# An eight-stage GNN, expert, LSTM and attention kernel: attention weights chosen by address, softmax sums by a ones column, query tiles outside; four more LSTM matmuls per cell issued ahead

## The reference

```
logits = sel_in @ W_sel.T + b_sel
onehot = one_hot(argmax(logits), 4)
g = einsum('bsg,bs->bg', g_all, onehot)
h2, c2 = _lstm_activate(g, c)
```

```
logits = relu(x.mean(axis=1) @ r_w1 + r_b1) @ r_w2 + r_b2
sel = argmax(softmax(logits))
scores = einsum('bhqd,bhkd->bhqk', q, k) / sqrt(64)
out = einsum('bhqk,bhkd->bhqd', softmax(scores), v) ... @ wo
```

## Time and profile before

| | |
|---|---|
| runs, median (lowest to highest) | 5700.91 us (5697.95 to 5701.5) |
| the profiled execution's own time | 5706.91 us |
| its span | 5705.1 us |
| PE busy | 5027.5 us, 88% |
| DVE busy | 2837.5 us, 50% |
| ACT busy | 1437.0 us, 25% |
| LSTM steps | from about 2110 to 4963 us |
| attention and store | 5384 to 5705 us |

### The profile page before, as it was taken

One profiled execution on the slowest core, in us unless ns is written; L12 is line 12 of the kernel. 1 busy time (PEld: TensorE's weight loads), 2 busy tenths in 40 slices (PEclk: granted clock), 3 DMA queues, 4 the chain that ended last, 5 costly groups with the idle time before them and its releaser, 6 DMA issues. The chain is left out here.

```text
span 5705.1 us, 267215 instructions
## 1 busy us (share of the span) xinstructions
PE 5027.5 (88%) x109528; PEld 3080.5 (54%) x109528; DVE 2837.5 (50%) x11506; ACT 1437.0 (25%) x4745; POOL 633.6 (11%) x1073
## 2 busy tenths in 40 slices
PE   8899686899998989999999999999999999777688
PEld 6644343444565446666666666666666666554444
DVE  4501344232554755555555555555555555574533
ACT  0000000012332343333333333333333333242222
POOL 0000382000662110000000000000000000021000
PEclk9899897999999989999999999999999999898877
DMA  0000111166444740000000000000000000000200
GB/s 11 15 30 15 30 42 31 56 240 240 125 120 144 258 129 12 10 10 12 10 10 10 12 10 10 12 11 10 10 12 10 10 12 10 19 15 36 74 12 9
DMA packets 157671, 265.00 MB, mean 46 GB/s; under 512 B 48686, under 2 KB 83636, under 8 KB 153241
## 3 DMA queue, kind: packets, MB, share of 16 engines
q1 hardware_dynamic: 102548, 181.63, 9.6%
q0 software_dynamic: 55040, 82.30, 5.1%
HBM read 178.38 MB, written 85.14 MB: 46 GB/s over the span
## 5 line engine op out<-in xcount | busy, mean ns | idle before, releaser
L1558 PE MATMUL bank<-lstm_w,step_h_parts 128*32 128x128 f16 x87360 | 1453.8, 220 | 241.8 <-issue 241.8
L1558 PEld LDWEIGHTS bank<-lstm_w,step_h_parts 128*32 128x32 f16 x87360 | 1238.4, 97 | 613.3 <-issue 349.3
L1629 DVE TRANSPOSE_TENSOR_REDUCE step_summed<-bank 128x4 f32 (+1 forms) x2500 | 792.4, 317 | 1085.2 <-PE bank L1558 914.5
L1553 PE MATMUL bank<-step_xg,step_rows 128*128 (+1 forms) x2500 | 757.7, 385 | 45.1 <-DMA step_xg<-lstm_xg 18.8
L1526 ACT ACTIVATE step_act_out<-step_summed,lstm_inv_scale 128x4 f32<-128x4 f32 x625 | 185.8, 297 | 1724.1 <-DVE step_summed L1629 1724.1
L1514 POOL COPY xnT<-step_state 128x4 f32 (+1 forms) x625 | 116.7, 187 | 2759.9 <-DVE step_state L1654 2759.9
L1179 PE MATMUL bank<-sum_parts,sum_hot 125*125 125x512 f16 x1600 | 346.9, 380 | 6.7 <-DVE sum_parts L1138 6.7
L1179 PEld LDWEIGHTS bank<-sum_parts,sum_hot 125*125 125x125 f16 x1600 | 219.0, 137 | 135.0 <-DVE sum_parts L1138 7.5
L1429 PE MATMUL bank<-xg_w,xnT 128*125 128x512 f32 x640 | 276.6, 595 | 6.7 <-DMA xg_w<-in_c_w_ih 6.7
L538 POOL DMA_INDIRECT gcn_rows<-gcn_h_rows,gcn_idx x160 | 202.5, 1265 | 703.3 <-issue 703.3
L1553 PEld LDWEIGHTS bank<-step_xg,step_rows 128*128 128x128 bf16 x2500 | 142.5, 97 | 167.7 <-issue 129.8
(11 more groups left out here) (370 smaller groups left out, 6369.6 us busy)
## 6 DMA issues: line engine op xcount, KB each, us to landing
rel_h<-rel_h_sb SPq DMA_DIRECT2D x39, 1024.0 KB, 6.4
lstm_xg<-cnt POOLq DMA_DIRECT2D x80, 375.0 KB, 3.7
step_xg<-lstm_xg SPq DMA_DIRECT2D x375, 80.0 KB
xg_w<-in_c_w_ih SPq DMA_DIRECT2D x16, 1024.0 KB
lstm_w<-in_c_w_hh SPq DMA_DIRECT2D x16, 1024.0 KB, 11.6
cheb_w<-in_L_gnn_weight SPq DMA_DIRECT2D x8, 1024.0 KB
choose_we<-in_L_ffn_experts SPq DMA_DIRECT2D x8, 1024.0 KB
rel_bases<-in_L_gnn_bases SPq DMA_DIRECT2D x8, 1024.0 KB, 11.4
```

What stands on the lines that cost most here:

```text
L1553: return nc.tensor.matmul(bank[:], rows[:, p, :], xg[:, at, :], start=True, stop=stop)
L1558: last = nc.tensor.matmul(bank[32 * q:32 * q + 32, 128 * s:128 * s + 128], h_parts[:, c, :], w[:, s, c, q, a, 128 * p:128 * p + 128], star ...
L1629: nc.vector.tensor_reduce(summed[:, 4 * p:4 * p + 4], bank[:, bass.ds(s * 128, 128)].rearrange("p (b r) -> p b r", r=32), X_AXIS, ALU.add, ...
```

## The change

**LSTM.** 32 matmuls instead of 16 are issued before the choice: both halves of the first h piece, for each cell. The chosen cell then has 120 left instead of 124. `inject_i_o` moves behind them.

**Attention.** The three candidates of each weight are laid out on the host as one array, widened to 8 heads (`c_wq`, `c_wk`, `c_wv`, `c_wo`). SP waits for the index, loads it into a register and fetches only the chosen matrices, k first. One-hot, mixing and ring are gone. `v` gets a 65th column of ones for each head, so that `sum_values(i)` (ten passes with 65 columns for each tile) gives the row's sum beside its values. `expo` no longer sums, `normalize` is gone, and `keep_sums` divides 64 columns by the sum behind the matmul. Query tiles are the outer loop, heads the inner one. Each query tile is turned, projected, added and stored while the next runs; `store` as a stage is gone.

```diff
 def cell(s):
     for part in parts:
-        for c, a in halves[1 if part is part_f else 0:]:
+        for c, a in halves[2 if part is part_f else 0:]:
...
 last.then_inc(score_done, 1)
-inject_i_o(t)
 pe.wait_ge(h_lo_ready, t)
 for s in range(CELLS):
-    add_half(part_f, s, 0, 0, stop=False)
+    for a in range(2):
+        add_half(part_f, s, 0, a, stop=False)
+inject_i_o(t)
 pe.wait_ge(picked, 1)
```

```diff
-TILES = [(hd, m) for hd in range(AH) for m in range(NT)]
+TILES = [(hd, m) for m in range(NT) for hd in range(AH)]
+P_SLOTS = 3
...
 # sync
-for n, (w, i) in enumerate(PAIRS):
...
+sp.wait_ge(picked, 1)
+e = sp.value_load(pick[0:1, 0:1], min_val=0, max_val=NK - 1)
+def load(name, dst, loaded):
+    sp.dma_start(dst[:], I[name].rearrange("e (c p) n -> p (e c) n", p=128)[:, bass.ds(e * KC, KC), :]
+                 ).then_inc(loaded, 16)
+load("c_wk", wk, wk_loaded)
+load("c_wq", wq, wq_loaded)
+load("c_wv", wv, wv_loaded)
+load("c_wo", wo, wo_loaded)
+for m in range(NT):
+    sp.wait_ge(added, m + 1)
+    sp.dma_start(B.out_rows[:, m, :], B.x[:, m, :]).then_inc(out_stored, 16)
+sp.wait_ge(out_stored, 16 * NT)
...
 # vector
-def normalize(i):
...
+def keep_sums(i):
+    hd, m = TILES[i]
+    s = slice(i % 4, i % 4 + 1)
+    dve.wait_ge(o_done, i + 1)
+    nc.vector.reciprocal(inv[:, s], sums[:, DK:DK + 1]).then_inc(inv_ready, 1)
...
+    nc.vector.tensor_scalar(o[:, m % 2, hd * DK:(hd + 1) * DK], sums[:, 0:DK], inv[:, s], None, ALU.mult
+                            ).then_inc(o_kept, 1)
+for i in range(M + 1):
+    if i < M:
+        keep_turned(i)
+    if i + 2 < M:
+        row_max(i + 2)
+    if i >= 1:
+        keep_sums(i - 1)
+    if i >= AH and i % AH == 6:
+        add_out(i // AH - 1)
...
 # tensor
-def sum_head(hd):
...
+def sum_values(i):
+    hd, m = TILES[i]
+    pe.wait_ge(pT_kept_a, i + 1)
+    pe.wait_ge(pT_kept_v, i + 1)
+    if i >= 1:
+        pe.wait_ge(o_kept, i)
+    for t in range(NT):
+        last = nc.tensor.matmul(sums, pT[:, i % 2, t, :], v[:, t, hd, :], start=(t == 0),
+                                stop=(t == NT - 1))
+    last.then_inc(o_done, 1)
+def turn_out(m):      # four transposes of o into bank 7
...
+def project(m):
+    pe.wait_ge(oT_kept, m + 1)
+    for c in range(KC):
+        last = nc.tensor.matmul(B.bank[7][0:R, :], oT[:, m % 2, c, :], wo[:, c, :], start=(c == 0),
+                                stop=(c == KC - 1))
+    last.then_inc(out_done, 1)
+for i in range(M + 1):
+    if i < M:
+        turn(i)
+    if i + 2 < M:
+        scores(i + 2)
+    if i >= 1:
+        sum_values(i - 1)
+    if i >= AH and i % AH == 2:
+        turn_out(i // AH - 1)
+    if i >= AH and i % AH == 4:
+        project(i // AH - 1)
```

More of the change, by code:

```diff
@@ L2188, in _ @@
[L2188 to L2205, removed]
+            nc.vector.max_index(pick[:], best[:], score[:]).then_inc(picked, 1)
@@ L2246, in _ @@
-            for i in range(M + 2):
-                if i >= 2:
-                    keep_turned(i - 2)
-                    if (i - 2) % NT == 1 and i - 2 > NT:
-                        keep_out((i - 2) // NT - 1)
-                if 1 <= i <= M:
-                    normalize(i - 1)
-                if i < M:
-                    row_max(i)
-            keep_out(AH - 1)
-            for m in range(NT):
-                dve.wait_ge(out_done, m + 1)
-                nc.vector.tensor_tensor(B.x[:, m, :], B.x[:, m, :], B.bank[m % 4][0:R, :], ALU.add
-                                        ).then_inc(added, 1)
+            def keep_turned(i):
+                dve.wait_ge(p_turned, i + 1)
+                if i >= 2:
+                    dve.wait_ge(o_done, i - 1)
+                nc.vector.tensor_copy(pT[:, i % 2, 4, :], turn_tail).then_inc(pT_kept_v, 1)
@@ L2278, in expo @@
[L2278 to L2281 removed]
+                if i >= P_SLOTS:
+                    act.wait_ge(p_turned, i - P_SLOTS + 1)
@@ L2306, in _ @@
+            expo(1)
+            for i in range(M):
+                keep_turned(i)
+                if i + 2 < M:
+                    expo(i + 2)
+                if i >= AH and i % AH == 2:
+                    keep_oT(i // AH - 1)
+            keep_oT(NT - 1)
         @block.tensor
@@ L2378, in _ @@
+            def project(m):
+                pe.wait_ge(oT_kept, m + 1)
+                for c in range(KC):
+                    last = nc.tensor.matmul(B.bank[7][0:R, :], oT[:, m % 2, c, :], wo[:, c, :], start=(c == 0),
+                                            stop=(c == KC - 1))
+                last.then_inc(out_done, 1)
             scores(0)
             scores(1)
-            for i in range(M):
-                turn(i)
+            pe.wait_ge(v_kept, NT + 1)
+            pe.wait_ge(wo_loaded, 16)
@@ L2382, in _ @@
+            for i in range(M + 1):
+                if i < M:
+                    turn(i)
                 if i + 2 < M:
                     scores(i + 2)
-                if i % NT == 0 and i > 0:
-                    sum_head(i // NT - 1)
-            sum_head(AH - 1)
-            pe.wait_ge(o_kept, 2 * AH)
-            pe.wait_ge(w_mixed, 4 * NK)
-            for m in range(NT):
-                if m >= 4:
-                    pe.wait_ge(added, m - 3)
-                for c in range(KC):
-                    last = nc.tensor.matmul(B.bank[m % 4][0:R, :], oT[:, c, m * R:(m + 1) * R], wmix[:, 3, c, :],
-                                            start=(c == 0), stop=(c == KC - 1))
-                last.then_inc(out_done, 1)
@@ L2398, in store @@
-def store(nc, ctx, B, out):
-    stored = nc.alloc_semaphore("out_stored")
-    with nc.Block() as block:
-        @block.sync
-        def _(sp):
-            sp.dma_start(out.rearrange("(j p) d -> p j d", p=R), B.x[:]).then_inc(stored, 16)
-            sp.wait_ge(stored, 16)
+                if i >= 1:
+                    sum_values(i - 1)
+                if i >= AH and i % AH == 2:
+                    turn_out(i // AH - 1)
+                if i >= AH and i % AH == 4:
+                    project(i // AH - 1)
@@ L2407, in program @@
+            turn_out(NT - 1)
+            project(NT - 1)
 def program(nc, I, out):
@@ L2417, in program @@
                 stage(nc, ctx, B)
-        store(nc, ctx, B, out)
 def lay_out(inputs):
@@ L2443, in lay_out @@
     out["c_xg_rows"] = rows
+    for name in "qkvo":
+        ws = [out.pop(f"L3_ffn_w{name}{i}") for i in range(3)]
+        out["c_w" + name] = np.stack([np.repeat(w.reshape(512, -1, 64), 512 // w.shape[1], 1).reshape(512, 512) for w in ws])
     w = out.pop("L2_ffn_W_sel")
```

188 lines of the change are left out of this document (78 added, 110 removed).

## The result

The changed kernel takes 5623.2 us (median of four runs, 5618.8 to 5623.8), against 5701.2 in the same session (5698.0 to 5705.0): a ratio of 0.986 with a 95% interval of 0.9845 to 0.9876, 78 us less. The forecast was 5644, with a range of 5600 to 5690. The profiled execution is the fastest of the four: 5618.8, span 5617.0, 88.1 less than the span before.

| part | before | after | difference | forecast |
|---|---|---|---|---|
| stages ahead of the LSTM | 1788.8 | 1782.7 | -6.1 | 0 |
| LSTM with its preparation | 3180.5 | 3164.5 | -16.0 | -5 |
| graph attention | 404.0 | 400.8 | -3.2 | 0 |
| attention, up to the first scores | 105.1 | 78.8 | -26.3 | -27 |
| loop and projection | 213.2 | 184.7 | -28.5 | -17 |

What follows compares the result with a forecast made beforehand. LSTM steps wait for the choice, and TensorE bounds the attention loop at a mean clock of 0.70. Terms -27 - 17 - 8 - 5 = -57 take the profiled 5706.9 to 5650, median 5644 us, range 5600 to 5690.

Steps and rivals of the forecast that it cites:

- Weights by address, -27: Attention before the loop: fetching only the chosen weights starts scores at 5451.5 instead of 5478.4, -27 us (-21 to -28).
- The bound on the other side: Attention weight fetch: k could take the store's 11.3 us if sharing queues with the other three; 5.3 was kept.
- The loop, -17: Attention loop and projection: 1.2 GHz until project(0), then 2.4 GHz held; 196.1 us against 213.1, -17.
- the price of the tile: Attention loop: turn, scores and sums of one tile take 3.47 us at 2.4 GHz or 6.07 at 1.2 GHz.
- The store, -8: End of attention: only a fifth of the output lands behind the last projection, 5.5 us instead of 13.5, -8 (-6 to -9).
- The LSTM, -5: LSTM steps: all gain 0.056 us, cell 0 loses 0.13 to the injection; -10 and +5 make -5 us.
- The +5 for a later register load: LSTM: TensorE's load of the choice comes some 0.01 us later a step behind 34 matmuls, another +5 us.
- Rival 1: Attention loop: 2.4 GHz from the start, loop 161.5 us, -92 in sum, 5609; chance 0.15.
- Rival 2: LSTM: the injection hides after all, so every step gains the full 0.056 us, 5614; chance 0.07.
- Rival 3: Attention loop: clock goes up and down as before, mean 0.70, loop 228.7 us, -24 in sum, 5677; chance 0.10.
- Rival 4: Attention loop: 1.2 GHz in all tiles, loop 274.5 us, +21 in sum, 5722, slower; chance 0.08.
- Rival 5: LSTM: the choice's register load is held up behind 34 queued matmuls, +75 us in sum, 5776, slower; chance 0.06.

Runs made afterwards that it cites:

- experiment 6: Changed kernel with no turned output or projection inside the loop, all five behind the last tile: 5700.8 us (0.9996).
- experiment 5: Changed kernel with scores 0 and 1 issued ahead of the value projection: 5585.5 us (0.9791).
- experiment 3: Changed kernel with gate i injected before the wait for the split h, only gate o behind the 32 advance matmuls: 5613.5 us (0.9844).
- experiment 11: Edits of experiment 3 and experiment 5 together on the changed kernel, plus VectorE lowering its four gate semaphores between the same step's reductions: 5565.6 us (0.9761).
- experiment 4: Changed kernel with both injections before the wait for the split h, the 32 advance matmuls last before the choice: 5644.2 us (0.9903).
- experiment 7: Changed kernel with scores 0 and 1 ahead of the value projection and all projections behind the loop: 5591.8 us (0.9804).

## Why the prediction was right, step by step

- *Weights by address, -27:* measured -26.3, and -26.3 alone. The bound on the other side, a landing of 11.3 if the four shared the queues, did not come: k took 5.4.
- *The loop, -17:* measured -28.5. The course of the clock was as the step on it said: down in the second turn, up in project(0), then held. The first turn waited until 3.6 behind the first scores (3.5). What failed is the price of the tile: 3.47 forecast at full clock, 3.08 measured, and 6.07 against 5.82. The scores' 1.48 were read from one start to the next in the earlier trace rows, where the next turn has a wait of 0.17 for normalizing in its bracket. That wait was on the list of what the change removes, and should have been taken off: 1.31, against 1.24 measured. The sums were estimated at 1.25 with 0.2 for the change of operation, and are 1.15; the turn is 0.69 instead of 0.74. Up to the end of project(0) it is 4 less than forecast, behind it 7 less, although the clock fell behind the last value sums, which the forecast did not have. That TensorE has no gap was the step's reason for holding 2.4 GHz. It is no reason for reaching it: in experiment 6 TensorE had next to no gap either, and stayed at 1.2.
- *The store, -8:* -8.0. The last fifth landed in 3.7, for which 3.5 was taken.
- *The LSTM, -5:* -16, alone 16.9. The injection stood in the way of cell 0 and of no other cell, as forecast. Two terms were mis-sized. The first load of cell 0 came 0.116 later, not 0.13, and a step of it lost 0.049, not 0.074; the other cells gained 0.057 to 0.060, near the 0.056. That makes 9.5 - 17.1 - 7.6 = -15, and the first two steps took 1 less: -16, where -10 was forecast. The +5 for a later register load came to nothing: 0.040 behind the choice, before and after.
- *Rival 1* (2.4 GHz from the start) was not what the change does, but experiment 5 made it so: 5585, where the rival, with its too dear tiles, said 5609. *Rival 2* (the full gain in every step) is what experiments 3 and 11 bring back, 10 and 6 us. *Rival 3* is what the old loop does, not the new one. *Rival 4* (1.2 GHz in all tiles) is experiment 6: 5701, where 5722 was worked out with dearer tiles; its chance of 8% rested on project(0) raising the clock, which was the right hinge. *Rival 5* (a register load held up by the queue) did not happen, because the two wide injections, not the 32 small loads, stand last; experiment 4, with the small ones last, shows a part of it, 0.064 a step.

Of the 21 us between the forecast and the median, 11 are the loop's tile and 11 the LSTM's terms; the forecast's other two terms were within 1.

## What to carry to other kernels

Where a stage's work cannot by itself raise or lower the granted clock, what stands at its entry decides it for the whole stage: put a long run of full-width matmuls, which has to be done anyway, into the first wait rather than ahead of it. When a price is read from the starts of two rows, take off the idle time in the bracket, above all if the change removes its cause. And when a gain shows in full on one engine but only in part in the step, look at which other engine starts from the same choice.

## What was not expected of the hardware

- The clock had two stable courses over the same 40 tiles: 0.50, with TensorE busy for 227 of 229 us, and 1.00, with TensorE busy for 121 of 122 us. The kernels' times are 109 us apart (experiments 6 and 7).
- Behind an injection over the whole array the first 32-column weight load starts 0.31 after the last injected matmul has begun (medians): in steps of cell 0 in the changed kernel, and before the advance loads in the kernel before, where the wait for the choice covered it.
- Semaphore decrements on VectorE, 0.093 each, were enough to lengthen a step of 4.4 us by 0.035 (experiment 11).
- TensorE's sequencer passed 32 small weight loads far enough ahead that the register load started 0.25 before the last of them was issued, and yet 0.064 later behind the choice than with the two injections last (experiment 4).
